# Slot comparison in two halves of four tiles, one ahead of the step's first turn of table loads and one behind it

## What is computed

```python
def gnn(x, src, edge_attr):                      # x is layer-normed
    node_feat = relu(x @ W_down.T + b_down)                   # nodes x 64
    time_feat = relu(edge_attr @ W_time.T + b_time)           # edges x 64
    sums   = segment_sum(time_feat, src, num_segments=n)
    counts = segment_sum(ones, src, num_segments=n)
    combined = concat([node_feat, sums / max(counts, 1)])
    return x + relu(combined @ W_fusion.T + b_fusion) @ W_up.T + b_up
x = x + gnn(layernorm(x), src, edge_attr)
x = x + shared_mlp(layernorm(x)) + top2_of_4_experts(layernorm(x))
```

## Time and profile before

| | us |
|---|---|
| median of 3 runs | 2625.97 |
| lowest and highest | 2618.89, 2632.24 |
| span of the profiled execution | 2387.8 |
| PE busy | 2163.3 (91%) |
| DVE busy | 1819.8 (76%) |
| ACT busy | 1324.4 (55%) |
| POOL busy | 1222.2 (51%) |

### The profile page before, as it was taken

One profiled execution on the slowest core, in us unless ns is written; L12 is line 12 of the kernel. 1 busy time (PEld: TensorE's weight loads), 2 busy tenths in 40 slices (PEclk: granted clock), 3 DMA queues, 4 the chain that ended last, 5 costly groups with the idle time before them and its releaser, 6 DMA issues.

```text
span 2387.8 us, 76843 instructions
## 1 busy us (share of the span) xinstructions
PE 2163.3 (91%) x28773; PEld 1798.7 (75%) x28773; DVE 1819.8 (76%) x5481; ACT 1324.4 (55%) x2833; POOL 1222.2 (51%) x944
## 2 busy tenths in 40 slices
PE   5778887789999999899999998888879999999998
PEld 1666665588988888799999998778756666676676
DVE  9987664687888987699998886899956656666565
ACT  1667776677878777777777776000023434344343
POOL 0787887888887888777788777000011111111110
PEclk7888988899999999999999999999989999999999
DMA  2263535456766666677777775777721111111111
GB/s 77 87 165 123 155 116 144 151 166 188 213 200 202 182 189 182 191 223 219 207 224 220 220 218 164 209 206 208 207 66 47 54 40 57 44 40 60 41 40 36
DMA packets 244429, 345.06 MB, mean 145 GB/s; under 512 B 34526, under 2 KB 218516, under 8 KB 243352
## 3 DMA queue, kind: packets, MB, share of 16 engines
q1 hardware_dynamic: 201252, 228.82, 35.0%
q0 software_dynamic: 42576, 110.49, 13.9%
q10 hardware_dynamic: 234, 0.85, 0.1%
HBM read 200.75 MB, written 186.38 MB: 162 GB/s over the span
## 4 chain that ended last, share of the span: by engine, by line
PE 60%; DMA 12%; issue 8%; DVE 8%; POOL 5%; ACT 4%; DVEq 2%; SPq 0%; POOLq 0%; ACTq 0%
PE bank L640 13%; PE moved L611 11%; PE bank L727 9%; DMA table<-arena 7%; PE moved L740 6%; PE bank L597 5%; POOL table L1564 4%; DMA arena<-table 4%; PE bank L615 3%; PE bank L735 2%; ACT arena L1378 2%; PE bank L813 2%; PE bank L769 2%; DVEq L1034 2%; ACT arena L1372 1%
## 5 line engine op out<-in xcount | busy, mean ns | idle before, releaser
L1564 POOL DMA_INDIRECT table<-arena x832 | 1093.8, 1315 | 338.7 <-issue 275.9
L1378 ACT ACTIVATE arena<-moved 128x588 bf16<-128x588 f32 x832 | 546.0, 662 | 193.3 <-PE moved L611 117.5
L611 PE MATMUL moved<-arena 128*128 128x196 bf16 x4992 | 602.5, 258 | 11.9 <-ACT arena L1378 10.8
L611 PEld LDWEIGHTS moved<-arena 128*128 128x128 f16 x4992 | 460.8, 99 | 94.8 <-ACT arena L1378 29.0
L1372 ACT ACTIVATE arena<-bank 128x512 f32<-128x512 f32 x624 | 372.2, 596 | 153.6 <-PE bank L597 124.9
L1127 DVE TENSOR_TENSOR arena<-arena 128x3072 f16<-128x3072 f16 x208 | 364.6, 1753 | 113.7 <-PE moved L611 112.4
L1051 DVE TENSOR_TENSOR sums<-sums,bank 128x130 f32 x912 | 259.0, 284 | 133.2 <-PE bank L640 120.3
L640 PE MATMUL bank<-arena 128*128 128x65 bf16 x8208 | 312.8, 194 | 34.7 <-DVE arena L1031 16.5
L640 PE MATMUL bank<-arena,w_all 128*128 128x65 bf16 x8208 | 309.9, 193 | 19.5 <-DVE sums L1051 10.1
L640 PEld LDWEIGHTS bank<-arena 128*128 128x128 bf16 x8208 | 290.7, 98 | 41.7 <-DVE arena L1031 30.3
L640 PEld LDWEIGHTS bank<-arena,w_all 128*128 128x128 bf16 x8208 | 288.3, 98 | 25.8 <-issue 12.9
(11 more groups left out here) (223 smaller groups left out, 2867.2 us busy)
## 6 DMA issues: line engine op xcount, KB each, us to landing
arena<-table SPq DMA_DIRECT2D x304, 441.0 KB
arena<-in_attr SPq DMA_DIRECT2D x208, 144.0 KB
table<-arena POOLq DMA_INDIRECT x832
x_ln<-arena SPq DMA_DIRECT2D x98, 128.0 KB
arena<-in_x SPq DMA_DIRECT2D x97, 128.0 KB
arena<-x_ln SPq DMA_DIRECT2D x24, 512.0 KB, 4.6
out_rows<-arena SPq DMA_DIRECT2D x24, 512.0 KB, 3.3
fused_node<-arena SPq DMA_DIRECT2D x98, 32.0 KB
```

The source lines that it names most:

```text
L611: mm = e.matmul(moved8[:, 4 * (n % 2) + h, 0:PW], slot_hot[s % NSLOT][:, t, h * P:(h + 1) * P], upper(s, 0, PW)[:, t, :], start=j == 0, st ...
L1378: e.activation(row_buf[n % NROWS], moved8[:, 4 * (n % 2):4 * (n % 2) + 3, 0:PW], ACT.Copy).then_inc(s_rows, 1)
L1564: e.indirect_dma_start(out=tables[k], out_offset=bass.IndirectOffsetOnAxis(ap=dest[s % NDEST][:, a:a + 1], axis=0), in_=row_buf[n % NROWS] ...
```

## The change

The slot comparison is cut in two of 1536 elements. `one_hots` makes begun and the half for the first four tiles; a new function `slots(s, half_of)` makes a half. In a step DVE now runs `one_hots(s + 1)` ahead of the first turn and `slots(s + 1, 1)` behind it. s_slot counts two for a step, and PE waits for the second half ahead of its third move.

```diff
                 if a == 0:
                     e.wait_ge(s_low, s + 1)
                     e.wait_ge(s_lo, s + 1)
-                    e.wait_ge(s_slot, s + 1)
+                    e.wait_ge(s_slot, 2 * s + 1)
+                if a == GS // 2:
+                    e.wait_ge(s_slot, 2 * s + 2)
...
                 if s >= NSLOT:
                     e.wait_ge(s_moved, GS * (s - NSLOT + 1))
-                code8 = codes.rearrange("p g j u -> p (g j) u")[:, s * TS:(s + 1) * TS, :]
-                e.tensor_tensor(in_pairs(slot_hot[s % NSLOT]), pairs(iota_16, TS), each_pair(code8, BLOCK * P), ALU.is_equal).then_inc(s_slot, 1)
+                slots(s, 0)
+
+            def slots(s, half_of):
+                t0, n = half_of * (TS // 2), TS // 2
+                code4 = codes.rearrange("p g j u -> p (g j) u")[:, s * TS + t0:s * TS + t0 + n, :]
+                e.tensor_tensor(in_pairs(slot_hot[s % NSLOT][:, t0:t0 + n, :]), pairs(iota_16, n), each_pair(code4, BLOCK * P), ALU.is_equal).then_inc(s_slot, 1)
 
             one_hots(0)
+            slots(0, 1)
             for step in range(n_steps):
                 s = step
                 turns = turn_at.get(step, [])
+                if s + 1 < NS:
+                    one_hots(s + 1)
                 for k, n in turns[:1]:
                     turn(k, n)
                 if s + 1 < NS:
-                    one_hots(s + 1)
+                    slots(s + 1, 1)
```

## The result

In the comparison that decides this case the changed kernel takes **2652.09 us** (median of 5 runs, 2642.72 to 2654.63), before **2625.97 us** (5 runs, 2618.89 to 2632.24): ratio **1.0106**, 95% interval 1.0077 to 1.0134. The change makes it slower by 1.1%; the prediction said 2598 us, faster by 1%, with a range up to 2632.

A forecast was written before the change was run, and what follows sets the result against it. It took POOL's scatters, held by DVE's comparisons, to limit PE up to 985 us, and full PE to bound 985 to 1485. Terms +2 + 4 - 15 - 15 - 4 = -28 us, from 2625.97 to 2598 us; range 2566 to 2632.

The forecast's parts named there:

- the sentence under the sum: Whole kernel: 238.2 us between profiled span 2387.8 and median 2625.97 lie outside the trace and stay unchanged.
- The mechanism: Steps up to 985 us: a comparison holds POOL's scatter until it ends; two halves cost 41% less than one whole.
- +2 - 4: 55 to 227 us: +2 us for more DVE work, -4 us (0 to -7) for shorter scatter holds.
- 41% of the holds: 227 to 461 us: 27 waits, 25 us; 41% is the low bound, 10 us, high bound 22; taken -15 us.
- the class near 2.37 us: Scatters of 227 to 461 us in the profile after: this duration class should be gone, mean 1.15 us or less.
- One rival: Queue faster, PE not; POOL may not get between adjoining halves from 227 to 461 us: 2618 us, chance 0.27.
- 25.9 as the cap: 461 to 985 us: -15 us (0 to -25) from shorter holds, capped by PE's 25.9 us wait for this chain.
- forecast 0: 985 to 1485 us: POOL gains as much but PE is full, so 0; after 1485 us nothing changes.
- The move (+4): Steps with turns, from 56: begun and first half delay the first turn by up to 1.3 us; three episodes, +4 us.
- DVE's halves: Slot comparison on DVE: each half of 1536 elements takes 952 ns, adding 0.06 to 0.15 us a step.
- Scatters blocking comparisons: DVE, 208 more comparisons: running scatters hold them, 80 us lost, a third on the path; 2640 us, chance 0.03.
- The rival "slower": Steps with two turns: the first turn comes up to 1.3 us late, about 20 steps lost; 2642 us, chance 0.08.

The follow-up runs named there:

- e1: The kernel before, unchanged, run and profiled once more against before at the long level (2662.82 us): ratio 0.9978.
- e5: The changed kernel once more against before, at the short level: 2339.48 us against 2386.62, ratio 0.9795.
- g1: Split alone, both halves behind the first turn, against before at the short level (2388.16 us): ratio 0.9871.
- g2: Move alone, begun and the whole comparison ahead of the first turn, against before at the short level (2388.16 us): ratio 0.9892.
- e6: Only begun ahead of the first turn, whole comparison behind it, against before at the short level (2386.62 us): ratio 0.9902.
- e3: Move alone, begun and the whole comparison ahead of the first turn, against before at the long level (2662.82 us): ratio 1.0163.
- f2: Two matmuls instead of three for each one-hot of a table sum, against before at the long level (2655.82 us): ratio 0.9791.
- e7: Before's order, four of eight tiles compared from the third step on, against before at the short level (2386.62 us): ratio 0.9618.
- e11: Before's order, four of eight tiles compared from the third step on, against before at the long level (2657.64 us): ratio 1.0170.
- g3: 110 more scatters in the last turns and two matmuls instead of three, against before at the short level (2388.16 us): ratio 1.0068.

## Why the prediction was wrong, point by point

**The step that failed** is the sentence under the sum: "the 238.2 us between are outside the trace's first and last instruction and stay". In no timed execution do more than 1.9 us lie outside. The time stood inside the steps, as the trace at the long level (e1) shows: 1765.9 us to the last move against 1485.0. That is a level that the prediction's trace did not show, and all that the prediction says on what bounds the kernel ("POOL has no free time", PE at 498.90 of 500) is true of the short level only. A gap of a tenth between span and median was the warning, and it was explained instead of followed up: what the trace doesn't hold can't be argued to stay. With it the sum put a term at nothing that the trace could not show, PE's pauses: 170 us in after against 134 in e1, 88 against 67 inside add_up.

**The mechanism was right, at the level of its trace.** There the change gives 47 us of 2387, forecast 28. By stretch, before against e5:

- *Up to step 21:* -4.9 us (232.9 to 228.0), forecast +2 - 4.
- *Steps 22 to 55:* -12.0 us (239.1 to 227.1), forecast -15 by 41% of the holds. The scatters' mean there fell from 1.26 to 1.18 us (155.25 / 132), not to 1.15 or less; the class near 2.37 us is gone, as said. Step 56 begins 17 us earlier, forecast 15 to 20. g1 shows that it is the split: the halves follow each other directly and scatters do get in between. One rival said they would not.
- *Steps 56 to 131:* -26.3 us (500.4 to 474.1), forecast -15 with 25.9 as the cap; but the reason was another than given. The split brings 5 of it (g1), the place 20 (g2, e6).
- *From step 132 on:* -4.6 us, forecast 0, and -2.4 in the last turns.
- *The move (+4):* wrong in sign. Expected was that DVE's turn would come late. PE hardly waited for a late turn (6.4 us for sums in all steps, e5), and begun ahead of the turn gained 20 us from step 56 to 131 where the text had nothing to gain. Without these 20 us the total would have been near the forecast of 28; with them it is 47. Why is not settled: from step 56 to 131 DVE's wait for PE's chunks at L1051 fell from 64.6 us to 43.1 (e6), and PE's wait at L615 from 23.1 to 12.5 (e6) and 10.7 us (g2). That fits begun filling a time in which DVE idled, and in e6 also two separate holds in place of one of 2.2 us; no run tells these apart.
- *DVE's halves:* 0.95 us each (416 in after, below), as worked out from the earlier trace rows.
- *Scatters blocking comparisons (chance 0.03):* again not seen. The Trainium skill ("SBUF — State Buffer", Who interferes with whom) has the exclusion in either direction; the measurement decides, and shows one. 416 halves of after lie between 940 and 1019 ns, though POOL is in a scatter half of the time:

```profile
L1133 DVE TENSOR_TENSOR arena<-arena x416: 940/953/1019, 59.8 to 1738.2; 128x1536 f16<-128x1536 f16 x139
```

**At the long level** the mechanism worked on the engines it named, and the measured time went the other way. Scatters got shorter (mean from 1268 to 1145 ns from step 56 to 131, 1275 to 1130 behind it), PE waited 58 us less for ScalarE at the identity product (46 less with the moves), and PE paused 36 us more, 20 of it inside add_up. These don't add up to a loss. Between the two traces the balance from step 56 to 131 still is a gain, 616.6 us in e1 and 605.0 in after; from step 132 on it is a loss, 624.1 to 629.9: PE's wait behind ScalarE was short there already (9.7 us in e1), little was left to win, and the pauses rose from 56 to 64 us. The profiled execution of e1 belongs to a comparison that runs 1.4% longer than the one of after, so a difference of a few us between the two traces proves nothing; that the change is slower rests on the ratio of its own comparison. So the 1.1% is measured, and the runs show that work ahead of the turn costs at this level and comes with more stops at add_up (e3: 41 us more); a full account of the 26 us they do not give.

The rival "slower" that the prediction carried (DVE's turn becomes the bound) is not what came: PE waited 6.4 us in three waits for sums up to step 207 at the short level (e5), and at the long one these waits are not among after's seven longest.

**What stays open.** What a scatter takes from PE: the pauses come where PE takes in instructions fastest (two in 32 ns), with a third fewer instructions there (f2) the stops at add_up fell from 74.7 to 28.1 us in the steps and vanished from the last turns, and table loads don't matter in the steps. A supply of instructions that scatters disturb would fit, but it is not shown, and the run meant to test it was made at the other level. Open too: why scatters pause PE in some comparisons and not in others (the DMA packets of the scatters are as many and take as long, 125 ns on average in e1 and in the first trace), what makes the pauses more in the move and with half a comparison but not in the split, which part of the move costs at the long level (begun alone in front, e6, was run at the short one only), and why the level changes at all. What fills the 281 us between the levels is in the traces: 126 us are pauses, and about 123 us are PE itself, busy longer with the same matmuls. PE's columns over the steps, the first trace and then e1:

```profile
62.00:1485.00 1423.00, 1292.89 (x19580) 1153.65 (x19578) 1150.43 (x2900) 1059.55 (x2369) 1134.20 (x865) 0.96 0.63 182
62.00:1766.00 1704.00, 1415.47 (x19579) 1223.23 (x19577) 1153.29 (x2899) 1066.43 (x2370) 1082.83 (x865) 0.92 0.51 152
```

Of these, 46 us are in add_up (400.72 against 446.31 us for 10,368 matmuls). Part of it is the clock: 321 us of the steps ran at the lower of its two levels (1.2 GHz) in e1 and 154 us in the first trace; PE was busy 84% of the 617 us from step 56 to 131 in the one and 94% of 500 in the other.

No order of these instructions that was run beat before at both levels. At the short one the changed kernel is the fastest complete one; at the long one it is before.

## What to carry to other kernels

Hold the span of the profiled execution against the runs that are to be predicted, before reading a single row: where they differ by more than a per cent or two, the trace shows another kernel than the one that is timed, and the bound has to be argued for both. A saving can be real in its mechanism and still be given back by what it sets free; leaving out half of the instruction in question (e7, e11) gives an upper price and its sign in one run, at the level at which it is made. And an engine's stops without a releaser are a class of their own: sum them by place, keep apart those before an instruction that waits for a semaphore, and hold their starts against the other engines' instructions.

## What the runs showed of the hardware

- At the long level a row scatter (0.97 us on POOL) can make PE stop inside add_up for 0.2 to 0.6 us, once or twice, mostly 0.2 to 0.6 and 0.8 to 1.4 us after it began, though no semaphore is waited for; 110 scatters added 50 pauses of 0.2 us or more. At the short level no trace has a pause inside add_up in the steps.
- The same program on the same chip runs at two levels 10 to 12% apart (2387 and 2626 to 2663 us), each steady for a whole comparison and each with its own granted clock (0.947 and more, 0.946 and less); an edit of DVE's work can have the opposite sign at each: -3.8% and +1.7% for the same half comparison.
- PE with two short instructions every 32 ns pauses now and then without a scatter beside it (11 to 19 us in 237 to 261 us of table sums, at both levels, in all kernels with three matmuls), in stops of 0.2 us or more hardly with small table loads, and not at all with matmuls of 65 and 128 columns in turn (f2, g3).
